# The first pass of two scan layers: constants on two queues and two semaphores, and six of twelve fills made within the pass

## The reference

```python
seq = x.reshape(B, C, L).transpose(0, 2, 1)              # B = 16, C = 192, L = 1024
proj = seq @ W_proj.T + b_proj
x_in, delta, Bm, Cm = split(proj, [192, 192, 16, 16])
A = -jnp.exp(A_log)                                      # 192 x 16
delta = jax.nn.softplus(delta + dt_bias)
# for t in 0..1023, with h of shape (channels, 16 states):
#   h = exp(delta_t * A) * h + (delta_t * x_t) * B_t
#   y_t = sum over states of h * C_t
out = (y + x_in * D) @ W_out.T + b_out
```

## Time and profile before

| | us |
|---|---|
| median of 3 runs | 4435.09 |
| lowest and highest | 4430.67, 4450.03 |
| the profiled execution, its own time | 4430.47 |
| its span, first to last instruction | 4428.7 |
| TensorE busy | 3952.5 (89%) |
| VectorE busy | 3265.2 (74%) |
| POOL busy | 2474.9 (56%) |
| ScalarE busy | 2111.4 (48%) |
| mean granted clock of TensorE, share of 2.4 GHz | 0.934 |

### The profile page before, as it was taken

One profiled execution on the slowest core, in us unless ns is written; L12 is line 12 of the kernel. 1 busy time (PEld: TensorE's weight loads), 2 busy tenths in 40 slices (PEclk: granted clock), 3 DMA queues, 4 the chain that ended last, 5 costly groups with the idle time before them and its releaser, 6 DMA issues.

```text
span 4428.7 us, 165322 instructions
## 1 busy us (share of the span) xinstructions
PE 3952.5 (89%) x71984; PEld 2430.5 (55%) x71984; DVE 3265.2 (74%) x3492; ACT 2111.4 (48%) x2771; POOL 2474.9 (56%) x877
## 2 busy tenths in 40 slices
PE   4994898998999984899999999999999999999998
PEld 4994566666666652455555555454454454544554
DVE  6655576665766751688888878888878888888786
ACT  2331444434444432555555555555555555555553
POOL 1121211212112110678888888888888888888887
PEclk9997999999999996789999999899999999999999
DMA  9624232423324221443544534535535435445343
GB/s 102 86 40 101 81 102 70 126 70 95 104 67 115 83 68 47 102 97 86 129 91 99 127 79 105 123 77 118 110 77 127 101 88 126 92 100 125 80 96 72
DMA packets 370756, 419.26 MB, mean 95 GB/s; under 512 B 31401, under 2 KB 283949, under 8 KB 370017
## 3 DMA queue, kind: packets, MB, share of 16 engines
q1 hardware_dynamic: 370050, 408.65, 40.8%
HBM read 267.06 MB, written 91.16 MB: 81 GB/s over the span
## 4 chain that ended last, share of the span: by engine, by line
PE 53%; issue 4%; DVE 2%; ACT 1%; SPq 1%; POOL 0%; DMA 0%; DVEq 0%; POOLq 0%; ACTq 0%
PE ssm_u_ps L789 19%; PE ssm_y_ps L802 16%; PE ssm_scratch L819 8%; PE ssm_scratch L853 6%; DVE ssm_h L1089 1%; PE ssm_scratch L829 1%; PE ssm_scratch L844 1%; DVE ssm_b_diag L1113 1%; SPq L723 1%; ACT ssm_o_sb L1004 1%; PE ssm_scratch L838 0%; PE ssm_scratch L809 0%; DVE ssm_stats L1096 0%; POOL ssm_h L1169 0%; DMA ssm_xn<-const_ones 0%
## 5 line engine op out<-in xcount | busy, mean ns | idle before, releaser
L1169 POOL TENSOR_TENSOR ssm_h<-ssm_h,ssm_c_rep 128x2048 f32<-128x2048 f32 x384 | 1741.9, 4539 | 210.4 <-DVE ssm_h L1089 195.3
L1089 DVE TENSOR_TENSOR_SCAN ssm_h<-ssm_decay,ssm_h,ssm_u_ps 128x512 f32<-128x512 f32 x768 | 945.6, 1259 | 270.0 <-PE ssm_u_ps L789 269.7
L789 PEld LDWEIGHTS ssm_u_ps<-ssm_b_diag,ssm_dx_t 32*64 32x64 f32 x49152 | 830.2, 139 | 569.7 <-issue 566.8
L789 PE MATMUL ssm_u_ps<-ssm_b_diag,ssm_dx_t 32*64 32x64 f32 x49152 | 935.7, 227 | 97.5 <-issue 82.9
L927 ACT ACTIVATE ssm_decay<-ssm_delta_rep,ssm_a_neg 128x1024 f32<-128x1024 f32 x768 | 856.6, 1142 | 320.6 <-DVE ssm_h L1089 317.6
L1089 DVE TENSOR_TENSOR_SCAN ssm_h<-ssm_decay,ssm_u_ps 128x512 f32<-128x512 f32 x768 | 888.9, 1198 | 94.2 <-PE ssm_u_ps L789 72.4
L802 PE MATMUL ssm_y_ps<-ssm_h,ssm_state_sum 128*64 128x512 f32 x3072 | 820.4, 657 | 13.3 <-issue 8.4
L1703 ACT ACTIVATE l_probs<-l_work 128x532 f32<-128x532 f32 (+1 forms) x384 | 217.3, 566 | 562.0 <-PE l_work L1557 555.3
L802 PEld LDWEIGHTS ssm_y_ps<-ssm_h,ssm_state_sum 128*64 128x64 f32 x3072 | 199.0, 145 | 292.7 <-issue 257.9
L1872 DVE RECIPROCAL l_den<-l_den 96x1024 f32<-96x1024 f32 x32 | 209.6, 6548 | 197.4 <-ACT l_den L1716 197.4
L1955 POOL TENSOR_TENSOR l_rstd<-l_var_eps,l_minus_half 96x2 f32<-96x2 f32 x16 | 11.1, 693 | 586.0 <-DVE l_var_eps L1792 586.0
(11 more groups left out here) (162 smaller groups left out, 5705.8 us busy)
## 6 DMA issues: line engine op xcount, KB each, us to landing
ssm_c_rep<-ssm_c_by_state SPq DMA_DIRECT2D x256, 512.0 KB, 6.7
ssm_delta_rep<-ssm_delta SPq DMA_DIRECT2D x384, 128.0 KB, 6.1
l_qk_parts<-l_qk SPq DMA_DIRECT2D x48, 768.0 KB, 4.8
ssm_x<-x_after_l SPq DMA_DIRECT2D x32, 768.0 KB, 6.1
ssm_x_res<-x_after_l SPq DMA_DIRECT2D x192, 128.0 KB
l_x<-x SPq DMA_DIRECT2D x64, 192.0 KB, 8.8
x_after_l<-l_x SPq DMA_DIRECT2D x64, 192.0 KB, 4.1
l_x<-x_after_l SPq DMA_DIRECT2D x16, 768.0 KB, 5.5
```

Of the source, the lines that this page charges most:

```text
L789: made = nc.tensor.matmul(u_ps[64 * par:64 * par + 64, w % U_RING, r - 2 * win, at:at + 64], dx_t[rows, n.s, db, k, 64 * g:64 * g + 64], b ...
L1089: nc.vector.tensor_tensor_scan(h[:, s % S_RING, npi, t], decay[:, 2 * (s % 2) + npi, t], u, start, ALU.mult, ALU.add).then_inc(scanned, 1)
L1169: nc.gpsimd.tensor_tensor(view, view, c_rep[:, 2 * q:2 * q + 2, :], ALU.mult).then_inc(c_applied, 1)
```

## The change

Two things, in the scan layers' first pass only. The 19 constants become 25 loads on two semaphores: the 97-row tiles are loaded as 96 rows and 1 row; 14 loads (`first_loaded`: the shared tables, both a_log, and layer L2's w_delta, w_bc, w_x and d_skip, and the ones) are awaited where all 19 were, and 11 (`rest_loaded`) only by the first projection out. Eight of the 14 are issued by ScalarE ahead of its wait. And the prologue makes six fills (norm, de.0, bc, x.0, bt, dx.0); de.1, x.1, dx.1, de.2, x.2 and dx.2 go to slots 0, 1, 4, 5, 6 and 8 of the pass, with their work on ScalarE, POOL and SP moved alike.

```diff
-    return {slot: [f for f in names if keep(f)] for slot, names in slots.items()}
+    order = {slot: [f for f in names if keep(f)] for slot, names in slots.items()}
+    if first:
+        for slot, name in FIRST_SLOTS.items():
+            order[slot] = [name] + order.get(slot, [])
+    return {slot: order[slot] for slot in sorted(order)}
...
-FIRST_FILLS = ["norm", "de.0", "de.1", "de.2", "bc", "bt", "x.0", "x.1", "dx.0", "x.2", "dx.1", "dx.2"]
+FIRST_FILLS = ["norm", "de.0", "bc", "x.0", "bt", "dx.0"]
+FIRST_SLOTS = {0: "own.de.1", 1: "own.x.1", 4: "own.dx.1", 5: "own.de.2", 6: "own.x.2", 8: "own.dx.2"}
...
-        N_CONSTS = 19
+        N_FIRST, N_REST = 14, 11
+
+        def of_slot(n, name):
+
+            if name.startswith("own."):
+                return n, name[4:]
+            return (before(n) if name.startswith("tail") else n if name in OWN else after(n)), name
...
                 def prologue(n):
                     load(n)
-                    for t, a in ((group_avg, consts["group_avg"]), (lane, consts["lane"]), (ident, consts["ident"]),
-                                 (state_sum, consts["state_sum"])):
-                        sp.dma_start(t[:], a).then_inc(consts_loaded, 16)
+                    sp.dma_start(group_avg[:], consts["group_avg"]).then_inc(first_loaded, 16)
+                    sp.dma_start(xn[C:C + 1, :, :, :], consts["ones"]).then_inc(first_loaded, 16)
+                    for t, a in ((w_delta, ws[0]["w_delta"]), (w_bc, ws[0]["w_bc"])):
+                        sp.dma_start(t[0][0:C], a[0:C]).then_inc(first_loaded, 16)
+                        sp.dma_start(t[0][C:C + 1], a[C:C + 1]).then_inc(first_loaded, 16)
+                    for t, a in ((w_delta, ws[1]["w_delta"]), (w_bc, ws[1]["w_bc"]), (w_x, ws[1]["w_x"])):
+                        sp.dma_start(t[1][0:C], a[0:C]).then_inc(rest_loaded, 16)
+                        sp.dma_start(t[1][C:C + 1], a[C:C + 1]).then_inc(rest_loaded, 16)
+                    sp.dma_start(d_skip[1][:], ws[1]["d_skip"]).then_inc(rest_loaded, 16)
                     for i, w in enumerate(ws):
-                        sp.dma_start(a_neg[:, i, :], w["a_log"]).then_inc(consts_loaded, 16)
-                        for t, a in ((w_delta, w["w_delta"]), (w_bc, w["w_bc"]), (w_x, w["w_x"]), (d_skip, w["d_skip"]),
-                                     (w_out, w["w_out"]), (b_out, w["b_out"])):
-                            sp.dma_start(t[i][:], a).then_inc(consts_loaded, 16)
-                    sp.dma_start(xn[C:C + 1, :, :, :], consts["ones"]).then_inc(consts_loaded, 16)
+                        sp.dma_start(w_out[i][:], w["w_out"]).then_inc(rest_loaded, 16)
+                        sp.dma_start(b_out[i][:], w["b_out"]).then_inc(rest_loaded, 16)
                     sp.wait_ge(xn_made, 1)
                     load(after(n))
                     load_delta(n, 0)
-                    load_delta(n, 1)
                     store_c(n)
                     sp.wait_ge(c_stored, 32)
                     load_c(n, 0)
                     load_c(n, 1)
-                    load_delta(n, 2)
 
                 def early(n):
                     load_c(n, 2)
                     load_c(n, 3)
                     if n.first:
+                        load_delta(n, 1)
                         load_residual(n)
-                    else:
-                        load_delta(n, 2)
+                    load_delta(n, 2)
...
                 def project_out(n, q):
...
                     if q == 0:
                         pe.wait_ge(y_kept, n.count(3, 3))
+                        if n.first:
+                            pe.wait_ge(rest_loaded, 16 * N_REST)
...
                 def prologue(n):
                     square_mean(n)
                     take_norm(n)
                     normalise(n)
-                    for db in range(3):
-                        take_delta(n, db)
+                    take_delta(n, 0)
                     take_bc(n)
+                    take_x(n, 0)
                     take_b(n)
-                    take_x(n, 0)
-                    take_x(n, 1)
                     take_dx(n, 0)
-                    take_x(n, 2)
-                    take_dx(n, 1)
-                    take_dx(n, 2)
                     exps(n, 0)
...
-                act.wait_ge(consts_loaded, 16 * N_CONSTS)
+                for i, w in enumerate(ws):
+                    act.dma_start(a_neg[:, i, :], w["a_log"]).then_inc(first_loaded, 16)
+                act.dma_start(ident[:], consts["ident"]).then_inc(first_loaded, 16)
+                act.dma_start(lane[:], consts["lane"]).then_inc(first_loaded, 16)
+                act.dma_start(w_x[0][0:C], ws[0]["w_x"][0:C]).then_inc(first_loaded, 16)
+                act.dma_start(w_x[0][C:C + 1], ws[0]["w_x"][C:C + 1]).then_inc(first_loaded, 16)
+                act.dma_start(d_skip[0][:], ws[0]["d_skip"]).then_inc(first_loaded, 16)
+                act.dma_start(state_sum[:], consts["state_sum"]).then_inc(first_loaded, 16)
+                act.wait_ge(first_loaded, 16 * N_FIRST)
...
                 def prologue(n):
                     power(n)
-                    for db in range(3):
-                        finish_delta(n, db)
-                    for db in range(3):
-                        make_dx(n, db)
+                    finish_delta(n, 0)
+                    make_dx(n, 0)
 
                 def step(n, s):
                     last = is_last(n)
+                    if n.first and s in (0, 3):
+                        finish_delta(n, 1 if s == 0 else 2)
+                    if n.first and s in (1, 4):
+                        make_dx(n, 1 if s == 1 else 2)
                     apply_c(n, s)
```

More of the change, by code:

```diff
@@ L548, in ssm_layers @@
         c_dram = nc.dram_tensor(f"{tag}_c_by_state", [2, 16, L], F32).ap()
-        consts_loaded = sem("consts_loaded")
+        first_loaded, rest_loaded = sem("first_loaded"), sem("rest_loaded")
         consts_made = sem("consts_made")
@@ L603, in fill @@
             per = len(MAIN_FILLS)
+            if n.first and name in FIRST_FILLS:
+                return Fill(0, 2 * per, FIRST_FILLS.index(name))
             if n.first and not name.startswith("tail"):
-                return Fill(0, 2 * per, FIRST_FILLS.index(name))
+                return Fill(0, 2 * per, len(FIRST_FILLS) + flat(slots(n)).index("own." + name))
             if name.startswith("tail"):
@@ L877, in make_slot @@
                     for name in slots(n).get(slot, ()):
-                        make(before(n) if name.startswith("tail") else n if name in OWN else after(n), name)
+                        make(*of_slot(n, name))
                 def prologue(n):
@@ L912, in tail @@
                         make(n, f"tail.{q}")
-                pe.wait_ge(consts_loaded, 16 * N_CONSTS)
+                pe.wait_ge(first_loaded, 16 * N_FIRST)
                 schedule(pe, prologue, early, late, tail)
@@ L1002, in take_output @@
                         act.wait_ge(res_added, n.count(3, 0))
+                    if q == 0 and n.first:
+                        act.wait_ge(rest_loaded, 16 * N_REST)
                     await_fill(act, f)
@@ L1007, in take_slot @@
                     for name in slots(n).get(slot, ()):
+                        of, name = of_slot(n, name)
                         kind, _, i = name.partition(".")
-                        of = n if name in OWN else after(n)
                         if kind == "norm":
@@ L1022, in take_slot @@
                         else:
-                            take_output(before(n), int(i))
+                            take_output(of, int(i))
                 def prologue(n):
@@ L1125, in prologue @@
                     channel_moments(n)
-                    dve.wait_ge(consts_loaded, 16 * N_CONSTS)
+                    dve.wait_ge(first_loaded, 16 * N_FIRST)
                     dve.wait_ge(consts_made, 2)
```

## The result

The changed kernel takes 4400.0 us (median of 8 runs, 4391.7 to 4415.4) where the kernel before takes 4433.3 (8 runs, 4422.3 to 4450.0): a ratio of 0.9922, with a 95% interval of 0.9902 to 0.9942, which is 26 to 43 us; the medians are 33 us apart. The profiled execution took 4395.34 us, its span 4393.5.

The account below looks back on a forecast made before the run. The start was taken as bound by 97-row loads on one DMA engine, then prologue fills through one bank at 1.2 GHz; 28.9 + 23.45 - 12.5 - 1 = 38.9, rounded to 38.5 us gained, gave 4395 us, range 4383 to 4411.

Parts of the forecast that it names:

- Part 1: Constants ahead of the prologue: TensorE starts at 1732.6 instead of 1761.5, 28.9 us gained, bounds 24 to 29.5.
- 1.34 million bytes at 256 GB/s: Constants: x and the constants ahead of or among the 14 loads take 5.2 us from 1724.4, so 1729.6.
- Rival (d): Constants: ACT's queue blocks like SP's, eight issues of 6.01 us, no change; chance 0.07 with (f) and like mishaps.
- Rival (f): Constants: the row cut does not spread the load, gain 10 us, 4424; chance 0.07 with (d) and like mishaps.
- The estimate beside the Trainium skill's rule: Constants: the second queue is worth at most eight issues, some 3.5 us; the rest of 28.9 is the row cut's.
- Part 2: Prologue cut to six fills: u fills start 23.95 us after TensorE's start instead of 47.4, 23.45 us gained.
- no projection of the prologue raises the clock: Prologue: its projections were taken to stay at 1.2 GHz, 3.68 us each, as in the profile before.
- Part 3: Six fills inside the first pass: 12.5 us lost plus 1 us for pauses; 82 to 86 us scan to scan.
- (a): First pass: the second y sum raises the clock, 5.3 us; 4405 with a second instruction stall; chance 0.17 including parts.
- (b): First pass: the clock rises during de.1, dx.2 comes 2 us sooner, 4393; chance 0.12 together with (c).
- Rival (c): First pass: the instruction stall and extra late waits vanish, 4.75 + 1 us more, 4389; chance 0.12 together with (b).
- (e): First pass: the clock stays at 1.2 GHz throughout, 54.4 us lost against 52.4 gained, 4440 with second stall; chance 0.02.

Follow-up runs that it names:

- e_cut: Kernel before with only the 97-row loads cut into 96 rows and 1 row, all on SP's queue and one semaphore; 4408.7 us, ratio 0.9933.
- e_queues: Kernel before with the two queues and two semaphores but without the row cut; 4427.5 us, ratio 0.9966.
- e_best: Changed kernel with C's copies after the first window's scans, 11 later loads held for the first 14, fourth b_diag multiply after window 1's scans; 4409.4 us, 0.9921.
- e_fills: Kernel before with only the six fills moved into the first pass, its 19 loads on one semaphore kept; 4431.4 us, ratio 0.9992.
- e_after_again: The changed kernel itself, run once more without any edit; 4402.5 us, ratio 0.9916.
- e_c_after: Changed kernel with SP holding all loads of C until the first window is scanned; 4395.6 us, ratio 0.9904.
- e_consts: Kernel before with only the constants' part (25 loads, row cut, two queues, two semaphores), all twelve fills left in the prologue; 4417.3 us, ratio 0.9949.
- e_c_late: Changed kernel with the last three quarters of C's copies held until the first window's scans; 4394.4 us, ratio 0.9905.
- e_warm: Changed kernel with idle matmuls, their results overwritten, between the prologue's fills; 4397.3 us, ratio 0.9898.

## Why the prediction was right, and where it was not

The forecast of 4395 (4383 to 4411) stands against a median of 4400.0, and a gain of 38.5 us against 33 in the medians. That the profiled execution, at 4395.34, is almost exactly the forecast is luck: in it the second pass started 40.9 us sooner after T0, 3.5 of them by a rise of the clock that was not forecast, T0 was 3.7 us earlier, and the other 31 passes took 9.3 longer. The mechanism was the one forecast, except for that rise. By its own steps:

**Part 1, constants: 28.9 forecast, 27.9 measured.** The mechanism is the one named; e_cut and e_queues show that the row count was the bound of most of it. The first 14 loads were all in at 1728.96, T0+9.5, when ScalarE, released by the last of them, touched a_neg; the statistics had ended a microsecond earlier. The forecast had the statistics as the later of the two. The missing 1 us lies in the term "1.34 million bytes at 256 GB/s": SP had issued the 11 later loads by 1726.3, while the first were still under way, and their bytes shared the engines, as e_best shows with 1.6 us. The forecast counted their issues and not their bytes. The price bounded without a row, ACT's issue of a load, came out at its short end (timeline of ScalarE's queue):

```profile
1721.38 0.47 ACTq L1085 DMA_DIRECT2D ssm_w_x<-l_w_x_in  x1
1721.88 0.54 ACTq L1086 DMA_DIRECT2D ssm_w_x<-l_w_x_in  x1
1722.44 0.36 ACTq L1087 DMA_DIRECT2D ssm_d_skip<-l_d_skip_in  x1
```

Rival (d), issues that block for 6 us, is refuted by these, and its counter-argument, that nothing is stuck on one engine any more, by the 5.41 us of e_queues borne out. Rival (f), a cut that does not spread, is refuted by e_cut. The estimate beside the Trainium skill's rule in the prediction, at most 3.5 us for the second queue and the rest for the cut, had no term for the second semaphore. On top of the cut, queue and semaphore together brought 4.2, so the rest, 23.7, is the cut's; the queue's own share was not measured.

**Part 2, the prologue: 26.55 us from first matmul to first scan forecast, 26.81 in e_fills, e_after_again and e_c_after.** Most of the small difference is in the wait between bc and x.0, which the walk took as 1.0 us where its row has 1.42; it was 1.33. Delta was made at P+13.7, P being the first matmul (13.8 forecast), and the first scan followed the last b_diag multiply, as forecast. In the profile after it was 23.36. The step that failed there is the sentence that no projection of the prologue raises the clock: bc and x.0 took 1.92 and 1.94 where the kernel before has 3.64 and 3.68, and the clock fell again just ahead of the u fills, at 1750.0. The rows of before were one execution, and the clock of that one was taken for a property of the code. It rose among the fills of the prologue in the profile after, in e_consts and in e_c_late, at T0+20.1 to 20.3, as de.0 ended, and not in e_cut, e_queues, e_fills, e_after_again, e_c_after and e_best; with idle matmuls it rose at T0+37.3 in both kernels, during the last idle matmul and 0.6 us ahead of the u fills. What decides it in one execution and not in the next stays open.

**Part 3, the first pass: 82 to 86 us forecast, 83.8 to 84.3 measured**, 13.2 us lost in the profile after and 13.7 in e_after_again, from scan to scan, where 12.5 + 1 from the start of the u fills comes to 13.0. The walk holds in its places: the first y sum began at F+25.3 (25.1 forecast, F the start of the u fills), POOL's apply_c(0), which it needs, had ended at F+20.5 (21.7 forecast), the clock rose 1.5 us after that y sum had ended, at F+30.5 where 28.8 was forecast (3.68 for the sum, 1.94 for the projection behind), and the next pass's de.0 ended at F+51.2 (49.6). The difference of 1.6 is about what the dx turn and the u fill behind the y sum took more, still partly at the low clock (1.12 and 1.34), the small pause of 0.71, and dx.2, which waited 1.13 for POOL instead of 0.7. POOL's two steps in question:

```profile
1765.01 1.27 POOL L1200 TENSOR_TENSOR ssm_delta<-ssm_relu,ssm_delta 128x512 f32<-128x512 f32 x1 [16.18 <-ACT ssm_delta L985]
1766.24 4.53 POOL L1190 TENSOR_TENSOR ssm_h<-ssm_h,ssm_c_rep 128x2048 f32<-128x2048 f32 x1
```

The pause was forecast as 4.75 for the first block and 1 in all for the later ones; it was 3.43 with 0.86 and 0.71 in the profile after, 5.05 with 0.66 in e_after_again. Its reading as instructions behind rows rested on one packet and is now shown by e_c_after and e_best. Rivals (a) and (b) are refuted: the rise came between the first y sum and the second, and not in de.1 (3.68 at 1758.80). Rival (c) is refuted with the pause, and (e), the low clock throughout, by the 0.96 from 1781.

**The sum.** At the low clock in the prologue the stages give 28.04 + 22.72 - 13.67 = 37.1 (e_after_again) where 38.9 was summed, and 40.9 in the profile after, where the clock rose. The medians give 33, within 26 to 43; both stage sums lie inside. What remains between them is put down to the spread of the other 31 passes, which no run tied to the change; only one execution of the kernel before was profiled, so that the change itself costs these passes a few us is not excluded.

## What to carry to other kernels

Look at the DMA share together with the GB/s: a share of one engine in 16 over a long stretch was here a tile of 97 rows, and cutting off the odd row was worth more (23.7 us) than a second queue and a second semaphore (4.2 on top). Bulk rows issued ahead of a block of new instructions held that block up here, and putting them off only moved the pause to the next block. When an edit is worth less than the passes behind it vary, compare the stage it touches between fixed events, and do so in more than one execution where the granted clock differs.

## What was not expected of the hardware

- The granted clock of one program in one stretch was 0.50 in one execution and 1.00 in another (prologue of the changed kernel, projections of 3.68 against 1.94 us), though TensorE's rows from the first matmul on agree up to there. Idle matmuls between the fills, 2.07 us each, did not bring the rise earlier than it came elsewhere by itself (T0+37 against T0+20).
- TensorE went on 2.6 to 3.1 us after the start of an instruction packet of 0.02 MB; the pause around it was 0.18 us with the DMA engines at 0.02 and 3.4 to 6.6 us with C's rows ahead of it (6.60 in e_warm, the engines at 1.03).
- The same remaining 31 passes took 2538.8 to 2570.3 us between the profiles, and in the one pass looked into, 7.8 us more went with a granted clock of 0.86 instead of 0.96.
